# Stage two of a cross-attention and expert feed-forward layer: rows and activations turned by VectorE and sixteen transfers in place of TensorE

## The reference

```python
x = x + tanh(g_xattn) * xattn(layernorm(x), ctx, ctx)     # stage one
xf = layernorm(x)
scores = xf @ Wr.T                                        # 1024 -> 64
top_vals, top_idx = top_k(scores, 16)
G = zeros.at[rows, top_idx].set(softmax(top_vals))
h = einsum('nd,krd->nkr', xf, A)                          # 1024 -> 64*16
out = einsum('nkr,kdr->nd', h * G[:, :, None], B) * 2.0
x = x + tanh(g_ffn) * out
```

## Time and profile before

| | |
|---|---|
| median of three runs | 960.5 us |
| the profiled execution | 959.67 us, its span 957.9 us |
| granted TensorE clock, mean | 0.994 of full speed (2.4 GHz) |
| busy: TensorE, weight loads, VectorE, ScalarE, GpSimd | 97%, 84%, 73%, 51%, 49% |
| chain that ended last | TensorE 81%, VectorE 10%, issue 5% |
| data moved | 88.31 MB, 92 GB/s on average |

### The profile page before, as it was taken

How to read it: one execution, slowest core, us unless ns; L and a number is a source line. 1 busy time by engine, 2 the same in 40 slices (tenths; PEclk the granted TensorE clock), 3 DMA queues, 4 the chain that set the end, 5 groups by cost and what they waited for, 6 DMA issues and landing times.

```text
span 957.9 us, 16074 instructions
## 1 busy us (share of the span) xinstructions
PE 932.2 (97%) x5084; PEld 800.5 (84%) x5084; DVE 704.0 (73%) x1532; ACT 492.2 (51%) x974; POOL 469.5 (49%) x323
## 2 busy tenths in 40 slices
PE   7899999999999999999999799999999999999998
PEld 5687887888888888888888699999999999999986
DVE  6888888888888888888888857766666666666521
ACT  4687786678768767876787634222222222222100
POOL 3775657678777877785787824222222111111100
PEclk9999999999999999999999999999999999999999
DMA  4226231231323113311312853121111111111001
GB/s 153 89 66 249 93 104 49 89 133 66 109 91 133 66 68 132 109 68 66 131 45 88 300 199 128 67 67 67 66 67 67 66 66 66 66 66 45 23 23 44
DMA packets 24805, 88.31 MB, mean 92 GB/s; under 512 B 3264, under 2 KB 3264, under 8 KB 24768
## 3 DMA queue, kind: packets, MB, share of 16 engines
q1 hardware_dynamic: 19296, 67.91, 19.9%
q0 software_dynamic: 5184, 19.40, 6.1%
q10 hardware_dynamic: 288, 0.52, 0.2%
HBM read 71.04 MB, written 16.78 MB: 92 GB/s over the span
## 4 chain that ended last, share of the span: by engine, by line
PE 81%; DVE 10%; issue 5%; ACT 1%; POOL 1%; DMA 1%; DVEq 0%; ACTq 0%; POOLq 0%
PE ps L61 22%; PE ps L63 22%; PE ps L62 22%; PE ps L1307 6%; PE ps L1298 4%; DVE qT_lo L909 3%; PE ps L1288 2%; PE ps L1402 1%; PE ps L1373 1%; DVE mt L933 1%; DVE ekT_lo L916 1%; DVE qmax L895 1%; DVE bn L831 1%; DVE kmax L889 1%; DVE qsum L900 1%
## 5 line engine op out<-in xcount | busy, mean ns | idle before, releaser
L471 POOL TENSOR_TENSOR rb<-u_in,rb 128x1024 f32<-128x1024 f32 x14 | 33.7, 2408 | 255.4 <-DVE rb L885 255.4
L400 POOL TENSOR_TENSOR qe<-qe,qrec 128x1024 f32<-128x1024 f32 x64 | 121.2, 1903 | 47.1 <-DVE qrec L903 47.1
L61 PE MATMUL ps<-aT_hi,yT_hi 128*128 128x448 f32 (+2 forms) x384 | 128.4, 334 | 5.4 <-issue 5.4
L63 PE MATMUL ps<-aT_lo,yT_hi 128*128 128x448 f32 (+2 forms) x384 | 126.6, 330 | 0.0
L62 PE MATMUL ps<-aT_hi,yT_lo 128*128 128x448 f32 (+2 forms) x384 | 126.5, 330 | 0.0
L909 DVE TENSOR_TENSOR qT_lo<-ps,qT_hi 128x512 fp32r<-128x512 f32 x128 | 82.4, 686 | 49.0 <-ACT qT_hi L628 48.5
L393 POOL TENSOR_TENSOR qhalf<-qe 128x512 f32<-128x512 f32 x64 | 82.2, 1284 | 64.8 <-ACT qe L620 61.8
L61 PE MATMUL ps<-bT_hi,hT_hi 128*128 128x512 f32 x256 | 102.6, 401 | 0.0
L63 PE MATMUL ps<-bT_lo,hT_hi 128*128 128x512 f32 x256 | 100.0, 391 | 0.0
L62 PE MATMUL ps<-bT_hi,hT_lo 128*128 128x512 f32 x256 | 99.8, 390 | 0.0
L700 ACT ACTIVATE hT_hi<-ps 128x512 fp32r<-128x512 f32 x32 | 19.1, 597 | 143.8 <-PE ps L1402 143.8
(11 more groups left out here) (155 smaller groups left out, 2397.5 us busy)
## 6 DMA issues: line engine op xcount, KB each, us to landing
x_in<-in_x SPq DMA_DIRECT2D x16, 512.0 KB, 4.4
ctx_in<-in_ctx SPq DMA_DIRECT2D x16, 512.0 KB, 4.9
ctxT_in<-in_ctxT SPq DMA_DIRECT2D x16, 512.0 KB, 3.4
ctxT_hi<-in_ctxT POOLq DMA_DIRECT2D x16, 512.0 KB, 3.8
u_scratch<-osb SPq DMA_DIRECT2D x16, 512.0 KB, 3.8
out<-res SPq DMA_DIRECT2D x16, 512.0 KB, 2.8
x<-in_x SPq DMA_DIRECT2D x15, 512.0 KB, 4.0
u_in<-u_scratch SPq DMA_DIRECT2D x14, 512.0 KB, 3.2
```

The lines of the kernel that those rows point to most:

```text
L61: nc.tensor.matmul(psum, whi, mhi, start=start, stop=False)
L63: return nc.tensor.matmul(psum, whi, mlo, start=False, stop=stop)
L400: nc.gpsimd.tensor_tensor(v, v, w, ALU.mult).then_inc(q_norm, 1)
```

## The change

In stage two TensorE no longer transposes y of batches 2 to 15 nor any hg. Instead:

- VectorE transposes the 32 x 32 blocks of the tile in place (`turn_y`, `turn_h`): of each block row and column change place, the blocks stay where they are.
- SyncE issues sixteen transfers of 32 partitions x 256 columns (`move_turned`), from SBUF to SBUF, which carry partition group a, column range q of the turned tile to partition group q, column range a of `y_raw` or `h_raw`. Afterwards feature 256q + 32m + i lies on partition 32q + i, for strip m. AT and BT are laid out by the same rule on the host (`strips`), and y of batches 0 and 1, which TensorE still transposes, is written with its columns in that order.
- High and low parts are then one pass over 1024 numbers each, from SBUF (`hi_moved_y`, `lo_moved_y`, `hi_moved_h`, `lo_moved_h`), where there were two over 512 from PSUM.
- `down(b)` is undivided except for batch 0, does all of half g = 0 and then g = 1, and follows `up(b+1, 2)`; `sum_u(b+2)` stands between pieces 0 and 1 of `up(b)`, its bank is another (`psN`).
- The load of `u` of b+3 waits for the landing of y's sixteen (`y_moved`) instead of TensorE's transposes; gating waits for `h_moved`.

The core of the diff:

```diff
+        MOVED = 16 * (P // 32) ** 2
+        def move_turned(queue, dst, src, s):
+            for a in range(P // 32):
+                for q in range(P // 32):
+                    queue.dma_start(dst[32 * q:32 * q + 32, 256 * a:256 * a + 256],
+                                    src[32 * a:32 * a + 32, 256 * q:256 * q + 256]).then_inc(s, 16)
+        def by_strip(raw):
+            return raw[:, :].rearrange("p (a m i) -> p m a i", a=P // 32, i=32)
+        def by_group(tile):
+            return tile[:, :, :].rearrange("p m (a i) -> p m a i", i=32)
```

SyncE's body b:

```diff
+                if not isinstance(i, int) or b <= NB - 2:
+                    sp.wait_ge(y_turned, b)
+                    move_turned(sp, y_raw, y[(j + 2) % 2], y_moved)
                 if not isinstance(i, int) or b <= NB - 4:
-                    sp.wait_ge(y_T, 2 * b + 4)
+                    sp.wait_ge(y_moved, MOVED * b)
                     load_u(b + 3, j % 2)
+                sp.wait_ge(h_turned, b + 1)
+                move_turned(sp, h_raw, hg, h_moved)
```

ScalarE's new steps:

```diff
+            def hi_moved_y(b):
+                act.wait_ge(h_mm, 3 * b)
+                act.wait_ge(y_moved, MOVED * (b - 1))
+                nc.scalar.activation(by_group(yT[0]), by_strip(y_raw), ACT.Copy).then_inc(y_hi, 2)
+            def hi_moved_h(b):
+                last = isinstance(b, int) and b == NB - 1
+                if last:
+                    act.wait_ge(h_mm, 3 * NB)
+                elif started(b):
+                    act.wait_ge(f_mm, 2 * b)
+                act.wait_ge(h_moved, MOVED * (b + 1))
+                nc.scalar.activation(by_group((hT_last if last else hT)[0]), by_strip(h_raw),
+                                     ACT.Copy).then_inc(h_hi, 2)
```

VectorE's new steps and, with the conditions on b left out, its body:

```diff
+            def turn_y(b, half):
+                dve.wait_ge(y_done, b + 1)
+                nc.vector.transpose(y[half][:, :], y[half][:, :]).then_inc(y_turned, 1)
+            def turn_h(b):
+                dve.wait_ge(hg_done, 3 * b + 3)
+                nc.vector.transpose(hg[:, :], hg[:, :]).then_inc(h_turned, 1)
...
                     result(b - 2, (j + 1) % 2, (j + 3) % SLOTS, 2 * i + (j - 1) // 2)
+                    lo_moved_h(b - 1)
                 part_u(b + 2)
+                turn_y(b + 1, j % 2)
                 route(b)
                 if first:
                     lo_b(4)
                     lo_b(6)
+                    lo_moved_h(0)
...
                     gated(b, p)
-                lo_y(b + 1)
-                lo_h(b, 0)
+                turn_h(b)
+                lo_moved_y(b + 1)
                 stats2(b + 2, (j + 3) % SLOTS)
```

TensorE's body, without the conditions on b (in body 1 `sum_u` stays behind `up(b, 2)`):

```diff
                 up(b, 0)
-                tr_h(b - 1, 1)
+                sum_u(b + 2)
                 up(b, 1)
                 up(b, 2)
-                sum_u(b + 2)
-                tr_y(b + 1, j % 2)
-                down(b - 1, 0)
-                tr_h(b, 0)
-                down(b - 1, 1)
+                down(b - 1)
```

More of the change, by code:

```diff
@@ L798, in _ @@
             hi_b(3)
-            hi_h(0, 0)
             def ffn_body(i, j):
                 b = SLOTS * i + j + 1
+                first = isinstance(i, int) and b == 1
+                if not first:
+                    hi_moved_h(b - 1)
                 if not isinstance(i, int) or b <= NB - 2:
                     normalise(b + 1, (j + 2) % SLOTS)
-                hi_h(b - 1, 1)
+                if first:
+                    hi_moved_h(0)
                 exp_scores(b)
                 if not isinstance(i, int) or b <= NB - 2:
-                    hi_y(b + 1)
-                hi_h(b, 0)
+                    hi_moved_y(b + 1)
                 if not isinstance(i, int) or b <= NB - 4:
@@ L1190, in _ @@
             gated(0, 2)
+            turn_h(0)
             lo_y(1)
@@ L1392, in up @@
                 last.then_inc(h_mm, 1)
-            def tr_h(b, g):
-                pe.wait_ge(hg_done, 3 * b + 2 + g)
-                if g == 1 or started(b):
-                    pe.wait_ge(h_lo, 2 * b + g)
-                else:
-                    pe.wait_ge(o_out, 2 * NB)
-                for n in range(4):
-                    w = (4 * g + n) * P
-                    last = nc.tensor.transpose(psG[:, n * P:n * P + P], hg[:, w:w + P], ident[:, :])
-                last.then_inc(h_T, 1)
@@ L1405, in down @@
-            def down(b, part_):
-                pe.wait_ge(h_lo, 2 * b + part_ + 1)
-                for g in range(2):
-                    if part_ == 0 and started(b):
-                        pe.wait_ge(res_done, 2 * b - 2 + g + 1)
-                    elif part_ == 0 and g == 0:
-                        pe.wait_ge(o_out, 2 * NB)
-                    v = slice(512 * g, 512 * g + 512)
-                    for m in range(KC // 2 * part_, KC // 2 * (part_ + 1)):
-                        if not started(b) and g == 0:
-                            wait_weight(pe, m)
-                        last = three_pass(psF[:, g, :], hT[0][:, m, :], hT[1][:, m, :], bT[0][:, m, v],
-                                          bT[1][:, m, v], m == 0, m == KC - 1)
-                    if part_ == 1:
-                        last.then_inc(f_mm, 1)
+            def down(b):
+                hi, lo = hT_last if isinstance(b, int) and b == NB - 1 else hT
+                first = isinstance(b, int) and b == 0
+                pe.wait_ge(h_lo, 2 * b + 2)
+                for strips in (range(KC // 2), range(KC // 2, KC)) if first else (range(KC),):
+                    for g in range(2):
+                        if first:
+                            pe.wait_ge(o_out, 2 * NB)
+                        else:
+                            pe.wait_ge(res_done, 2 * b - 2 + g + 1)
+                        v = slice(512 * g, 512 * g + 512)
+                        for m in strips:
+                            if first and g == 0:
+                                wait_weight(pe, m)
+                            last = three_pass(psF[:, g, :], hi[:, m, :], lo[:, m, :], bT[0][:, m, v],
+                                              bT[1][:, m, v], m == 0, m == KC - 1)
+                        if strips[-1] == KC - 1:
+                            last.then_inc(f_mm, 1)
```

86 lines of the change are left out of this document (47 added, 39 removed).

## The result

| | before | changed kernel |
|---|---|---|
| time, median of the runs shown side by side | 960.51 us (959.32 to 961.09) | 1018.19 us (1017.02 to 1018.55) |
| ratio, 95% interval | | 1.060 (1.0582 to 1.0618) |
| span of the profiled execution | 957.9 us | 1016.8 us |
| mean granted clock of TensorE over the span | 0.994 | 0.961 |
| start of `up` of batch 2, of batch 15 | 596.80, 918.74 | 606.13, 969.26 |

The account below looks back on a forecast made before the run. TensorE was taken to bound stage two. Span 957.9 + 6.15 (start) + 0.7 (batch 2) - 23.5 (periods) + 0 (end) = 941.2; adding 1.8 and 0.8 gave 943.8 us, range 935 to 978.

Parts of the forecast that it names:

- the price of an issue: SyncE's time to issue one small transfer: taken as 0.40 us, with 0.34 and 0.58 as low and high ends.
- D: Time from the end of a turn to the landing of its sixteen transfers: 7.9 us taken, 7.0 to 10.6.
- second ring: Loop through SyncE's queue, y's transfers, load of `u_in`, then h's transfers: 2D + 5.1, 20.9 us, hidden under 22.96.
- Rival (a): SyncE's queue: an issue costs 0.58, second ring 26.3, time 990 us; decides from 0.51 an issue; chance 0.17.
- TensorE's list: TensorE's work per stage-two batch: without transposes worth 1.81 us, the period falls from 24.77 to 22.96, saving 23.5.
- rival (b): VectorE becomes the bound: strided low parts cost 2.4 us, not 1.2; its list 24.6, time 965; chance 0.05.
- The lock between VectorE and GpSimd: y's low part slips between GpSimd's two residual passes; statistics begin 6.3 us behind the spread in place of 5.1.
- rival (c): Small transfers don't overlap, each at least 1.4 us: D = 22, second ring 49, time some 1300; chance 0.03.
- The start: Start of stage two: TensorE idles 6.5 us before `down(0)` at 590.1, then half clock; `up(2)` begins 6.15 later.
- The 0.7 for `sum_u` in batch 2: Body 2 of stage two: VectorE is still behind, so `sum_u(4)` waits for its sum of squares, +0.7 us.
- The end: After batch 15's `up` starts: hg transposes gone, -1.35 us; wait before `down(15)`, +1.3; together 0.
- both rings: Stage-two loops through D: first, h's transfers to routing and gating, D + 14.1, 22.0 us; second ring, 20.9; both hidden.

Follow-up runs that it names:

- the run with two queues: Changed kernel with half of each sixteen transfers issued by ScalarE, the other half by SyncE: 947.93 us, ratio 0.987 to the kernel before.
- the last kernel: Changed kernel with SyncE and ScalarE issuing, hg of batch 0 transposed by TensorE, sum of squares behind up's third piece in all batches: 939.59 us, ratio 0.978.
- h alone: Changed kernel with y transposed by TensorE again and only hg turned and moved by SyncE, sum behind up's third piece: 971.52 us, ratio 1.012.
- y alone: Kernel before with only y of batches 2 to 15 turned and moved by SyncE, hg still transposed on TensorE: 952.15 us, ratio 0.992.

## Why the prediction was wrong, step by step

**The step that failed is the price of an issue.** I wrote "I take an issue at 0.40, between a lone one and four in a row, since a quarter of the rows should cost no more than all". It is 0.63. The reason given was wrong twice: the number of rows has next to no weight (128 x 512, 32 x 256 and 32 rows of 64 bytes within SBUF are 0.64, 0.63 and 0.63), and the rows that it was taken from were loads from HBM and, for the lone 0.34, a store to it. The high end of the range, 0.58 from the row of eight, was also too low, and came from 544 KB a transfer, which these aren't. Its point of decision, 0.51, was not tried, but nothing speaks against it: 0.63 is well beyond it. Put into the prediction's own formulas, 0.63 gives D = 15 x 0.63 + 1.9 = 11.4 and a second ring of 27.9; measured are 12.0 for y, 11.4 for h and a ring of 28.3 to 28.5. Rival (a) had the mechanism and its place, and its 990 was still 28 us short (30 in the span): its ring was 26.3 in place of 28.3 to 28.5 (fifteen issues of h at 0.05 and fifteen of y at 0.08 too cheap, 1.9 together, and some 0.1 in each landing), which makes 21 over the thirteen periods; the start took 3.2 more and the end 5.7 more than it had.

**The chances.** What decided was a value outside both of its bounds, and each bound came from a transfer of another kind. A resource that gets thirty-two of something in a period, where before it had three, with a formula in which each counts twice, should not have held 0.17. Rival (a) also counted short: thirty-two issues a batch are four times the row of eight in the trace, not twice; it is the sixteen of one move that are twice.

**TensorE's list: right.** Period 22.96 forecast, 23.06 to 23.07 where nothing else binds; the transposes are worth 1.71 and not 1.81 a batch.

**VectorE: right.** High and low parts out of the strided `y_raw` and `h_raw` take 1.06 and 1.23, not 2.4: rival (b) is out. The list fits under 23.06 in every run with two queues. The lock between VectorE and GpSimd is there, if not in the form that I drew: in the run with two queues the low part of y took 1.96 on average and GpSimd's second pass 2.88, in place of 1.2 and 2.4. From its groups of instructions (count | busy, mean ns | idle before):

```profile
L503 POOL TENSOR_TENSOR x<-rb,x 128x1024 f32<-128x1024 f32 x14 | 40.3, 2878 | 2.0
...
L1092 DVE TENSOR_TENSOR yT_lo<-y_raw,yT_hi 128x1024 fp32r<-128x1024 f32 x14 | 27.4, 1956 | 2.8 <-ACT yT_hi L734 2.6
```

In the last kernel the statistics begin 5.9 behind the spread (756.57 to 762.48), for which I had 6.3.

**Overlap of the transfers: right.** They land 1.8 to 1.9 after their issue, one issue apart; rival (c), which the Trainium skill's figure for 64 KB (DMA: Bandwidth & Descriptors, Bandwidth; a load from HBM issued by GpSimd) would have supported if laid end to end, is out.

**The start: the stretch was right, its length was not.** Idle before `down(0)` 8.4 in place of 6.5, `down(0)` at 592.63 in place of 590.1. Left out was a queue: on ScalarE the exponentials of batch 1 stand behind the high part of h(0), which waits for the landing of h, and routing 1 on VectorE waits for them. Another 0.65 is TensorE's: from `down(0)` to `up(2)` it takes 13.5 where 11.0 + 1.85 stood. The two engines' timelines in the changed kernel:

```profile
586.81 1.06 ACT L743 ACTIVATE hT_hi<-h_raw 128x1024 fp32r<-128x1024 f32 x1 [7.01 <-DMA h_raw<-hg]
...
588.21 0.22 DVE L1044 TENSOR_TENSOR gsel<-gsel,ex 128x64 f32<-128x64 f32 x1 [4.52 <-ACT ex L748]
```

The sixteen issues of h(0) also took 12.05 there, 0.75 each, beside other traffic. The 0.7 for `sum_u` in batch 2 was right with two queues: that period was 23.76 against 23.06.

**The end: 8.4 more, 0 forecast.** D is 3.5 longer than taken (11.4, 985.2 to 996.6). In the changed kernel VectorE is late for the last batch, since the ring holds it: the last turn ends at 985.2, 3.9 behind the end of `up(15)` and not 1.85. And the result of batch 14 stands behind the low part of h(15) on VectorE, 0.7 that I didn't count. These three make the wait before `down(15)` 7.5 in place of 1.3; the other 2.2 or so are mostly the lower clock behind it (granted 0.50 from 999 to 1003). With two queues the wait before `down(15)` is 0.94, forecast 1.3, and the rest is as before: from `up(15)` to the end of the span 39.2 in both.

**With the issue corrected, does the rest of the sum hold?** With two queues D is about 7 (the last turn ends at 921.2, the high part begins at 928.1), below the 7.9 that the forecast took, and both rings are hidden as it demands. The span was then 946.6 against 941.2: 3.1 at the start, 1.3 for a period of 23.06, and 1.1 in batch 9 make 5.5. So the ledger was sound within 6 us but for the one term, and that term was worth 70.

## What to carry to other kernels

When a change hands work to a DMA queue, count its issues in a period, price them by a row of the same kind of transfer (which memory at each end), and write the rings that run through the queue; if no row of that kind is in the trace, measure one, as its price goes into the ring once for each move. Many small transfers belong on more than one issuing engine, or in fewer, wider ones, and the work that stands behind the issues on those engines has to be looked at too. A wait taken away at the head of a stage is worth something only when the next one behind it goes too: the transposes of batch 0 on TensorE gave 1.5 us by themselves, and together with the move of the sum of squares 8.3. What the sum's move gives without the transposes was not run.

## What the runs showed of the hardware that was not expected

- An issue costs SyncE 0.46 us for 32 x 256 across HBM and SBUF in either direction, and 0.63 to 0.65 within SBUF or within HBM; 2 KB, 32 KB, 64 KB and 256 KB within SBUF (32 x 16 to 128 x 512) all cost 0.62 to 0.64.
- SyncE's and ScalarE's queues issue side by side at 0.62 and 0.66. That doesn't slow SyncE's (0.63 alone); ScalarE's alone was not measured.
- VectorE has one long standstill of 2.95 to 4.3 us, with nothing that the profile shows, ahead of the results in batch 9, where the loop over batches enters its second round: 3.06 in the changed kernel, 2.95 with two queues, 3.1 in the last kernel, 3.6 with h alone, 4.3 with y alone, and only 0.47 in the kernel before. In the last kernel it is hidden, with two queues it costs TensorE 1.1 us, with y alone 1.6. Its cause wasn't tried. The row with two queues:

```profile
770.18 1.41 DVE L1114 SCALAR_TENSOR_TENSOR res<-ps,gf,x 128x512 f32<-128x512 f32 x2 [2.95 <-issue]
```
